# GpSimd's sum of squares moved between the two normalisations, and a stream of 206 slots written out instead of looped

## The reference

```
for i in range(6):
    x = attn_layer(shift_tokens(x), Wqkv[i], q_scale[i], k_scale[i], Wo[i]) + x
    x = ffn_layer(shift_tokens(x), ln_g[i], ln_b[i], W1[i], b1[i], W2[i], b2[i]) + x
# attn_layer
q = l2norm(q) * qs;  k = l2norm(k) * ksc          # per head of 64
q = q*cos*scale + rotate_half(q)*sin*scale;  k = k*cos/scale + rotate_half(k)*sin/scale
out = local_attention(q, k, v)                    # windows of 32, each sees itself and the one before
return out @ Wo
# ffn_layer
return a * gelu(gate) @ W2 + b2                   # a, gate = split(layernorm(x)*g + b) @ W1 + b1
```

## Time and profile before

| | us |
|---|---|
| median of 3 runs | 2080.57 (2078.74 to 2081.38) |
| the profiled execution | 2075.03 |
| its span | 2073.2 |

### The profile page before, as it was taken

The page is one execution under the profiler, slowest core; times in us unless marked ns, Lnnn a source line. Parts: engine busy times, 40 slices in busy tenths (PEclk is TensorE's granted clock), DMA queues, the critical chain, the costliest instruction groups (busy, mean ns, idle before and its releaser), DMA issues. The chain is left out here.

```text
span 2073.2 us, 70057 instructions
## 1 busy us (share of the span) xinstructions
PE 1919.3 (93%) x26905; PEld 1408.2 (68%) x26905; DVE 1605.8 (77%) x3109; ACT 1390.0 (67%) x2780; POOL 1341.2 (65%) x1402
## 2 busy tenths in 40 slices
PE   4999997899999999989989999998999899999995
PEld 3667665777767767767767677676777676777762
DVE  5666665788898878888868988688888788888773
ACT  2665663677757767776767577676777675777762
POOL 0000004998788767878767977688878678787840
PEclk9999999999999999999999999999999999999996
DMA  2000000443424334333343243343333433333330
GB/s 95 2 1 0 0 30 6 115 107 101 123 76 105 96 92 119 90 90 96 98 112 100 75 104 98 90 121 88 91 100 96 116 93 79 103 99 96 98 91 20
DMA packets 190633, 171.70 MB, mean 83 GB/s; under 512 B 32160, under 2 KB 186440, under 8 KB 190152
## 3 DMA queue, kind: packets, MB, share of 16 engines
q1 hardware_dynamic: 190280, 167.02, 30.7%
HBM read 21.14 MB, written 1.05 MB: 11 GB/s over the span
## 5 line engine op out<-in xcount | busy, mean ns | idle before, releaser
L407 POOL TENSOR_TENSOR z_raw<-rot_u,rot_v 128x256 f32<-128x256 f32 x768 | 552.2, 743 | 186.3 <-DVE rot_v L1016 183.8
L422 POOL TENSOR_TENSOR z_norm<-probs_t,z_raw 128x512 f32<-128x512 f32 x384 | 493.1, 1306 | 110.4 <-DVE probs_t L1065 110.4
L1015 DVE TENSOR_TENSOR rot_u<-bank,tabs 128x512 f32<-128x512 f32 x384 | 263.1, 685 | 183.3 <-ACT sq L521 180.2
L781 PE MATMUL bank<-x_high,w_high 128*128 128x256 f32 x768 | 304.4, 396 | 2.8 <-issue 1.1
L553 ACT ACTIVATE pair_bank<-pair_bank 128x512 f32<-128x512 f32 x192 | 111.8, 582 | 256.1 <-DVE pair_bank L998 255.9
L521 ACT ACTIVATE sq<-bank 128x512 f32<-128x512 f32 x384 | 225.6, 589 | 53.9 <-PE bank L783 44.4
L1016 DVE TENSOR_TENSOR rot_v<-bank,tabs 128x512 f32<-128x512 f32 x384 | 261.5, 681 | 0.0
L428 POOL TENSOR_TENSOR sqs<-sq 128x512 f32<-128x512 f32 x192 | 245.3, 1278 | 23.6 <-POOL z_norm L422 23.5
L540 ACT ACTIVATE probs_t<-bank 64x512 f32<-64x512 f32 x384 | 227.3, 592 | 45.4 <-PE bank L760 43.1
L772 PEld LDWEIGHTS bank<-probs_t,v_late 128*64 128x64 f32 x3072 | 155.5, 138 | 145.8 <-issue 145.8
L825 PE MATMUL bank<-sqs,consts 128*128 128x512 f32 x384 | 204.4, 614 | 44.5 <-POOL sqs L428 41.5
(11 more groups left out here) (153 smaller groups left out, 4545.4 us busy)
## 6 DMA issues: line engine op xcount, KB each, us to landing
zqk<-z_norm SPq DMA_DIRECT2D x1536, 64.0 KB, 2.1
v_late<-v_sb SPq DMA_DIRECT2D x192, 192.0 KB, 2.6
w_qkv<-in_L_ffn_Wqkv SPq DMA_DIRECT2D x18, 512.0 KB, 5.1
v_late<-v_sb SPq DMA_DIRECT2D x192, 32.0 KB, 2.2
wo<-in_L_ffn_Wo SPq DMA_DIRECT2D x24, 128.0 KB, 2.1
w<-in_L_ffn_W SPq DMA_DIRECT2D x12, 170.5 KB, 3.0
consts<-in_constants SPq DMA_DIRECT2D x1, 1088.0 KB, 5.1
w_qkv<-in_L_attn_w_kv_up SPq DMA_DIRECT2D x2, 512.0 KB, 6.3
```

The source lines that it names most:

```text
L407: a = pool.tensor_tensor(z_raw[:, parity, idx, half, :], rot_u[:, idx, half, :], rot_v[:, idx, 1 - half, :], ALU.add)
L422: a = pool.tensor_tensor(z_norm[:, parity, idx, :, :], rinv[:, idx, :].unsqueeze(1).broadcast_to([P, 2, T]), z_raw[:, parity, idx, :, :], ...
L781: pe.matmul(dst, w_high[:, j, cols], x_high[:, odd, :], start=True, stop=False)
L1015: dve.tensor_tensor(rot_u[:, idx, :, :], src, tabs[:, 2 * idx, :, :], ALU.mult)
```

## The change

Two edits. GpSimd's sum of squares of group s+4 goes between the key and the query normalisation of group s+3. And `stream` calls `slot(s)` for all slots from -4 to 205 with plain numbers, on all five engines: no loop register, no jump, waits on fixed counts, and the counting of `room_met` and `split_begun`, which only separated waits in the loop, is dropped. What is computed, the order of every other engine's instructions, and the transfers stay.

```diff
-        def stream(eng, slot):
-
-            for k in range(FIRST, LOOP):
-                slot(k, 0)
-            with eng.Fori(0, TURNS) as r:
-                for k in range(LOOP, LOOP + LAYER):
-                    slot(k, r)
-            for k in range(LOOP, LAST - TURNS * LAYER):
-                slot(k, TURNS)
+        def stream(slot):
+
+            for s in range(FIRST, LAST):
+                slot(s)
...
+        def layer_begun(s, at):
+
+            l, k = divmod(s - at, LAYER)
+            return l + 1 if k == 0 and 0 <= l < DEPTH - 1 else 0
...
+            def normalise(parity, idx):
+
+                return pool.tensor_tensor(z_norm[:, parity, idx, :, :], rinv[:, idx, :].unsqueeze(1).broadcast_to([P, 2, T]), z_raw[:, parity, idx, :, :], ALU.mult)
+
...
-                    for idx, summed in ((1, "k_summed"), (0, "q_summed")):
-                        pool.wait_ge(S[summed], m + 1)
-                        a = pool.tensor_tensor(z_norm[:, parity, idx, :, :], rinv[:, idx, :].unsqueeze(1).broadcast_to([P, 2, T]), z_raw[:, parity, idx, :, :], ALU.mult)
-                    a.then_inc(S["zn_ready"], 1)
+                    pool.wait_ge(S["bound_ready"], s + 4)
+                    after(pool, f"z_in{(s + 1) % G}", 16 * 2 * HG * ((s + 1) // G + 1))
+                    pool.wait_ge(S["k_summed"], s + 4)
+                    normalise((s + 3) % 2, 1)
                 if one:
                     pool.wait_ge(S["k_square"], s + 5)
                     pool.wait_ge(S["q_square"], s + 5)
                     after(pool, "n_done", s + 4)
                     pool.tensor_tensor(sqs[:, :, :], sq[:, :, 0, :], sq[:, :, 1, :], ALU.add).then_inc(S["sums_ready"], 1)
-                    rotated(s + 4, k % 2, 0, "q_prod", "q_summed")
...
+                if two:
+                    pool.wait_ge(S["q_summed"], s + 4)
+                    normalise((s + 3) % 2, 0).then_inc(S["zn_ready"], 1)
+                if one:
+                    rotated(s + 4, s % 2, 0, "q_prod", "q_summed")
```

More of the change, by code:

```diff
@@ L354, in slot @@
[L354 to L372, removed]
+                    out_weights(0, s + 1)
+                l = layer_begun(s, LAYER - 14)
+                if l:
+                    sp.wait_ge(S["split_done"], G * l)
+                    qkv_weights(l)
+                for g in range(G):
+                    l = layer_begun(s, LAYER - 1 + g)
+                    if l:
+                        sp.wait_ge(S["lwo_done"], s - 1)
+                        out_weights(l, g)
@@ L374, in _ @@
+            stream(slot)
             sp.wait_ge(S["scores_done"], GROUPS)
@@ L428, in slot @@
                     pool.tensor_tensor(sqs[:, :, :], sq[:, :, 0, :], sq[:, :, 1, :], ALU.add).then_inc(S["sums_ready"], 1)
-                    rotated(s + 4, k % 2, 0, "q_prod", "q_summed")
[L430 to L436, removed]
+                if two:
[3 more added lines that the diff above has]
+                    rotated(s + 4, s % 2, 0, "q_prod", "q_summed")
+                for g in range(G):
+                    l = layer_begun(s, LAYER - 7 + g)
+                    if l:
+                        pool.wait_ge(S["w_in"], 16 * 3 * (l + 1))
+                        pool.wait_ge(S["lv_done"], s + 4)
+                        split_weights(l, g)
             pool.wait_ge(S["pv_done"], STEPS)
@@ L442, in _ @@
                 split_weights(0, g)
-            stream(pool, slot)
+            stream(slot)
         @block.scalar
@@ L521, in squares, with slot @@
                 act.activation(sq[:, idx, :, :], src[:, :].rearrange("p (a t) -> p a t", a=2), ACT.Square).then_inc(S[mark], 1)
[L523 to L527, removed]
+            def slot(s):
+                g = s % G
+                one, two = active(s, -4, GROUPS - 4), active(s, -3, GROUPS - 3)
+                three, four = active(s, 0, GROUPS), active(s, 1, GROUPS + 1)
+                normed = g == 0 and active(s, 2 * G, 2 * G + GROUPS)
                 if two:
-                    m, og, odd = s + 3, (k + 3) % G, (k + 3) // G % 2
+                    m, og, odd = s + 3, (s + 3) % G, (s + 3) // G % 2
                     act.wait_ge(S["lv_done"], m + 1)
@@ L592, in slot @@
                     act.activation(gate[0:CW[2], 2, :], gate[0:CW[2], 2, :], ACT.Gelu).then_inc(S["gelu_done"], 1)
[L593 to L596, removed]
+                l = layer_begun(s, LAYER + 6)
+                if l:
+                    gains(l)
+                l = layer_begun(s, LAYER + 10)
+                if l:
+                    gate_biases(l)
             first_batch(causal, 0)
@@ L605, in _ @@
             act.wait_ge(S["spread_zero"], 2)
-            stream(act, slot)
+            stream(slot)
         @block.tensor
@@ L899, in _ @@
                 pt_taken(STEPS - 1, h)
-            stream(pe, slot)
+            stream(slot)
             for p in range(PAIRS):
@@ L1036, in out_biases, with slot @@
                 dve.wait_ge(S["out_bias_ready"], l + 1)
-            def slot(k, r):
-                s, g = LAYER * r + k, k % G
-                one, two, three = active(k, r, -4, GROUPS - 4), active(k, r, -3, GROUPS - 3), active(k, r, 0, GROUPS)
-                if k % (2 * G) == 5 and mlp_active(k, r, 21):
-                    p, b = mlp_of(k - 21, r), 2 * ((k - 21) // (2 * G)) % NB
+            def slot(s):
+                g = s % G
+                one, two, three = active(s, -4, GROUPS - 4), active(s, -3, GROUPS - 3), active(s, 0, GROUPS)
+                if mlp_slot(s, 21):
+                    p = (s - 21) // (2 * G)
+                    b = 2 * p % NB
                     dve.wait_ge(S["mlp_done"], p + 1)
@@ L1087, in slot @@
                     rotate(s + 4, 0, B_Q, "q_square", "q_summed", "q_prod")
-                if not isinstance(r, int) and k == LAYER - 5:
-                    rotary_tables(r + 1)
-                if not isinstance(r, int) and k == LAYER + 15:
-                    out_biases(r + 1)
+                l = layer_begun(s, LAYER - 5)
+                if l:
+                    rotary_tables(l)
+                l = layer_begun(s, LAYER + 15)
+                if l:
+                    out_biases(l)
             dve.wait_ge(S["latent_ready"], PAIRS)
@@ L1101, in _ @@
             turn(causal, 0, ("post",))
-            stream(dve, slot)
+            stream(slot)
             dve.wait_ge(S["mlp_res"], MLPS)
```

195 lines of the change are left out of this document (94 added, 101 removed).

## The result

The changed kernel took 2021.67 us (median of 4 runs, 2019.07 to 2030.91) against 2079.65 us for the kernel before on the same chip. The ratio is 0.9734, with a 95% interval from 0.9697 to 0.9772, so it is faster by some 55 us (58 between the two medians). A second measurement of the same kernel on another chip gave 0.9742 (0.9722 to 0.9762). The prediction was a saving of 39.8 us and a time of 2040.8, with a range from 2027 to 2053.

A forecast was written before the change was run, and what follows sets the result against it. TensorE, busy 64.7 of 66.6 us per eight slots, was taken as the bound. Loop 29.8 plus sum of squares 10.0 gave 39.8 us off the 2080.6 median, so 2040.8 us, range 2027 to 2053.

The forecast's parts named there:

- The loop, 29.8 us: Writing out the stream removes four loop jumps with their pauses and half-clock matmuls; 29.8 us saved, between 27.6 and 29.8.
- slower: Rival: written-out code pauses now and then for instruction fetch, costing the 160 formerly looped slots; 2100 us, chance 0.03.
- The pauses are not the jump's: Rival: slot 47's bias copy and weight load make the pauses, so the loop gives next to nothing; 2070.6 us, chance 0.05.
- only the loop pays: Rival: scores or VectorE's chain take up TensorE's freed time, so the reorder gives nothing; 2050.8 us, chance 0.14.
- The sum of squares, 10.0 us: GpSimd's sum starts earlier, so TensorE's norm matmul waits less; 10.0 us saved, from 4.4 to 14.1.
- the 16 ordinary waits of 0.36: In ordinary slots two behind the MLP's end, GpSimd is late; the earlier sum removes all 5.7 us of waiting.
- the start, 16 slots: At the stream's start GpSimd is slowest and its slot is not shortened, so the gain is 1.2 us once.
- The split slots, 0 of 4.1: In ten weight-split slots ahead of new rotary tables the wait goes, but GpSimd's unmoved end takes it back; 0 counted.
- a longer slot with the tables: Sign of being wrong: the slot with the new rotary tables takes longer than it did.
- The Gelu slots, 0 of 19.0: In 22 Gelu slots the sum waits for ScalarE's squares, not the query normalisation, so all 19.0 us of waits stay.
- What is later, costed at nothing: Query normalisation comes up to 3.4 us later in Gelu slots, covered by 9.2 us of slack before the scores; no cost.
- more than I count: Rival: Gelu slots gain after all, with split-slot waits and some restart half clock; 2025 us, 2009.3 at most, chance 0.08.

The follow-up runs named there:

- one_jump: Kernel before, GpSimd's order kept, with a loop of two 64-slot turns and the rest written out, leaving one jump of four; 2052.98 us, ratio 0.9891.
- squares_first: Changed kernel, with ScalarE squaring the queries ahead of the Gelu table load in Gelu slots; 2023.3 us, ratio 0.9763.
- loop_only: Kernel before with the stream written out and GpSimd's old order kept; 2046.92 us, ratio 0.9852; repeated on another chip, 2045.87 us, ratio 0.9844.
- experiment 5: Four kernels without new rotary tables for layers 1 to 5, looped or written out, old or new order; streams 1620.1, 1589.3, 1598.0, 1567.2 us.

## Why the prediction was right in kind and wrong in size

**The loop, 29.8 us: right.** The stream lost 30.4 us, 29.6 of it in the four jump slots and those behind them. The four gaps of over 3 us before L760 are gone (L749 now), the clock stays at 1.00 there, and the written-out slots show no pause without a releaser, so the rival "slower" has nothing for it. That register waits cost nothing was right too: ordinary slots took the same with and without loop, to within 1.6 us over the 147 slots that are neither at the start, nor at a jump, nor 25 to 28 of a turn. "The pauses are not the jump's" fell with `one_jump`, and "only the loop pays" with the 15 and 23 us that the order gave.

**The sum of squares, 10.0 us: the step that failed.** The mechanism was right: the sum comes earlier and TensorE stops waiting for it. What failed is the price. Each term was the trace's idle time before the matmul, which is not what a wait costs, and a gap of 0.1 us was put at nothing. The part measured 23.1 us. By kind of slot, both edits against the old order written out (means of two profiles each):

| term | predicted | measured |
|---|---|---|
| the 16 ordinary waits of 0.36 | 5.7 | 8.2 (0.51 each) |
| from the Gelu slot's norm matmul to the next, 22 | none | 6.0 (0.27 each) |
| the intervals one and five slots behind that one, 38 | none | 3.0 (0.08 each) |
| the start, 16 slots | 1.2 | 2.9 |
| slots 25 to 28 | 3.1 | 3.8 |
| all others | 0 | -0.8 |
| sum | 10.0 | 23.1 |

The 0.36 cost 0.51, for the reason shown under the result. The norm matmul behind the Gelu slot had in 22 places a gap of 0.11 us ahead of it, which I had not even counted as a wait; it cost 0.27. Both differ from the gap by about the 0.16 us found there. These two make 8.5 of the 13.1 us missing. The other intervals of 0.08 us had no wait for the sum before, and where they come from is open, as is the start, which differs by 1.5 us between the two profiles of the changed kernel. The range for this part, "with the split slots it is 14.1", took its upper end from the same column and so was too low as well.

**The split slots, 0 of 4.1, on the ground that the tables take it back: right in the loop only.** Of the two waits in each layer change the first (0.46) went, while the second (0.36) is 0.46 to 0.63 now; the slots 25 and 26 still give about 5 us over the five layer changes in every version. The tables' slot and the one behind it take nearly all of it back in the loop and about a quarter when written out. So that these four slots gave 3.8 us where 3.1 was forecast is luck: the 3.1 was to come from the waits behind the tables, and these two slots got 1.1 us longer, while the 5 us came from where none was forecast. The prediction had named a longer slot with the tables as a sign of being wrong, and that sign came. VectorE's bound, 1.67 us in the earlier trace rows, takes 0.42 there now. The tables behind it took longer in return, 8.34 us for the eight instructions where they had taken 7.31. The first row is the kernel before, the second the changed one:

```profile
876.55 7.31 DVE L1029 TENSOR_SCALAR tabs<-consts,par_rot 128x256 f32<-128x256 f32 x8
...
859.61 8.34 DVE L1018 TENSOR_SCALAR tabs<-consts,par_rot 128x256 f32<-128x256 f32 x8
```

GpSimd works all the while in both, and in the new order both normalisations of the slot lie beside the tables, where only the second did before. TensorE's wait in the tables' slot grew with it: 2.8 us for ScalarE's logarithm (L548), 1.77 before.

**The Gelu slots, 0 of 19.0: right.** 22 waits of 0.73 to 0.88 us stayed, and `squares_first` shows what stands behind them.

**What is later, costed at nothing: right.** No score matmul (L739, 0.0 us idle) waits for a transfer, although the query normalisation now starts 3.5 us after the end of the key normalisation in the Gelu slot shown above (975.08 against 970.34 + 1.27), where it had followed at once.

**The rival "more than I count"** named 2025 us, which is near the result, but by a mechanism that the runs deny: nothing came from the Gelu slots' own wait. The prediction also added the two parts up, each read from the looped kernel. Measured that way, 30.4 + 15.4 is 45.8 us and falls short of the 53.5 by the surplus of 7.7.

## What to carry to other kernels

Price a wait of TensorE from start to start, against a slot of the same kind that does not wait, not by the idle column; a gap of a tenth of a microsecond that returns every eight slots can be worth more than it shows. When an engine is nearly full, sort the slots by their place in the pattern and compare their intervals: this finds both the gain and what takes it back. Measure two edits in all four combinations before adding them up; here, the new order was worth 15 us in the looped stream and 23 in the written-out one.

## What the runs showed of the hardware

- A jump back of the loop cost 7.3 to 7.5 us on the mean on this five-engine program (four jumps 29.6 us in `loop_only` and its repeat, three 22.0 to 22.6 in `one_jump`), and the one left in `one_jump` 9.1. Of this, 3.0 to 4.2 was the first pause of TensorE and 0.3 to 2.1 a second one some instructions later, with a different length from jump to jump. Behind each jump the clock was at half for 6.8 us or more, and the rest of the cost is put down to that.
- Beyond the start of the stream, the clock fell to half only behind jumps and behind the tables' slots. In the two written-out kernels without tables it did not fall there once. Behind the tables' slots, in the new order, the six slots took 56.7 to 58.3 us, the longer the later a fall of 6.8 us began (the table under experiment 5).
- The eight instructions for the tables took 7.31 or 8.34 us for the same work, with GpSimd at work beside them, and a single one (128x256) up to 1.98 us. The same eight for layer 0, at 336.8 us in the kernel before with no GpSimd instruction running, took 2.19 us, the shortest 0.34. The Trainium skill, in "GPSIMD Engine Reference", section "Specifications", names contention of GpSimd with VectorE instructions that are in a two-port mode or have two SBUF inputs. The times here agree that GpSimd slows VectorE; which of the two cases the table instruction is, no run here shows.
